# First attention stage: three pairs of probability tiles added by DMA, eight GpSimd additions, one block of row sums, and a new order within the steps

## The reference, cut to what matters

```python
kv = cond @ wkv.T + bkv                       # cond: (4, 1601, 512)
k, v = jnp.split(kv, 2, axis=-1)              # 16 heads of 32 columns
attn = jax.nn.softmax(jnp.einsum('bnhd,bmhd->bhnm', q, k) * scale, axis=-1)
o = jnp.einsum('bhnm,bmhd->bnhd', attn, v).reshape(B, N, C)
out = _qdq(o) @ _qdq(wp).T + bp               # _qdq: fake quantisation to int8
```

## Time and profile before

| | us |
|---|---|
| median of 3 runs (2567.41 to 2570.51) | 2568.93 |
| span of the profiled execution | 2568.4 |
| TensorE busy | 2506.9 (98%) |
| VectorE busy | 1786.5 (70%) |
| GpSimd busy | 1286.9 (50%) |
| ScalarE busy | 1223.6 (48%) |

### The profile page before, as it was taken

The page is one execution under the profiler, slowest core; times in us unless marked ns, Lnnn a source line. Parts: engine busy times, 40 slices in busy tenths (PEclk is TensorE's granted clock), DMA queues, the critical chain, the costliest instruction groups (busy, mean ns, idle before and its releaser), DMA issues. The chain is left out here.

```text
span 2568.4 us, 33913 instructions
## 1 busy us (share of the span) xinstructions
PE 2506.9 (98%) x13273; PEld 1626.8 (63%) x13288; DVE 1786.5 (70%) x2456; ACT 1223.6 (48%) x1853; POOL 1286.9 (50%) x340
## 2 busy tenths in 40 slices
PE   8999999999999999999998999999999999999998
PEld 8988888987545545555544787788533333335786
DVE  4554554556777767777774676664899999999873
ACT  4222313311666666666664232322688888886110
POOL 0000000000999999999993000000599999997310
PEclk9999999999999999999999999999999999999999
DMA  8677776655535345354323754443997777776300
GB/s 303 212 255 236 265 283 240 221 172 160 115 83 121 68 96 108 68 111 93 68 71 137 246 185 156 155 164 87 245 213 168 167 159 167 159 170 196 120 33 33
DMA packets 218865, 405.10 MB, mean 158 GB/s; under 512 B 18217, under 2 KB 94537, under 8 KB 218641
## 3 DMA queue, kind: packets, MB, share of 16 engines
q1 hardware_dynamic: 218704, 402.93, 56.8%
HBM read 260.63 MB, written 140.59 MB: 156 GB/s over the span
## 5 line engine op out<-in xcount | busy, mean ns | idle before, releaser
L1486 POOL TENSOR_TENSOR pooled<-pooled,probs 128x2048 f32<-128x2048 f32 x140 | 641.5, 4582 | 21.0 <-POOL pooled L1486 0.9
L1345 ACT ACTIVATE probs<-psum 128x512 f32<-128x512 f32 (+1 forms) x832 | 449.6, 600 | 333.6 <-PE psum L1231 328.4
L1372 DVE TENSOR_REDUCE win_max<-psum 128x1 f32<-128x802 f32 x480 | 454.3, 988 | 133.9 <-PE psum L1196 133.6
L2271 DVE TENSOR_SCALAR probs<-psum,bound 128x1024 f32<-128x1024 f32 (+1 forms) x416 | 499.0, 1275 | 31.5 <-POOL pooled L2303 21.3
L2246 ACT ACTIVATE probs<-probs 128x1024 f32<-128x1024 f32 (+1 forms) x416 | 437.6, 1059 | 82.5 <-DVE probs L2271 40.6
L2303 POOL TENSOR_TENSOR pooled<-pooled,probs 128x2048 f32<-128x2048 f32 x92 | 424.2, 4611 | 13.2 <-ACT probs L2246 1.0
L1231 PE MATMUL psum<-q_st,k_st 128*128 128x512 f32 (+1 forms) x832 | 318.7, 436 | 22.2 <-ACT probs L1345 15.6
L312 POOL TENSOR_TENSOR r_q<-ve_q,minus_half 128x4 f32<-128x4 f32 x8 | 9.1, 1133 | 611.3 <-DVE ve_q L256 611.3
L1196 PE MATMUL psum<-k_st,q_st 96*128 96x402 f32 x960 | 265.8, 358 | 0.9 <-DVE o_sb L1391 0.4
L1231 PEld LDWEIGHTS psum<-q_st,k_st 128*128 128x128 f32 (+1 forms) x832 | 149.4, 185 | 180.4 <-ACT probs L1345 130.6
L2214 PE MATMUL psum<-q_st,k_st 128*128 128x512 f32 (+1 forms) x832 | 251.6, 428 | 10.7 <-DVE probs L2271 9.6
(11 more groups left out here) (276 smaller groups left out, 4211.1 us busy)
## 6 DMA issues: line engine op xcount, KB each, us to landing
k_st<-k_hi SPq DMA_DIRECT2D x64, 801.0 KB, 10.6
k_st<-k_lo SPq DMA_DIRECT2D x48, 801.0 KB, 11.1
k_hi<-kt_hi SPq DMA_DIRECT2D x32, 801.0 KB
k_lo<-kt_lo SPq DMA_DIRECT2D x32, 801.0 KB
v_rows<-v_out SPq DMA_DIRECT2D x96, 256.0 KB
v_st<-v_rows SPq DMA_DIRECT2D x24, 768.0 KB
q_st<-q_hi SPq DMA_DIRECT2D x64, 256.0 KB, 8.4
w<-w_hi_d SPq DMA_DIRECT2D x64, 256.0 KB, 3.1
```

Of the source, the lines that this page charges most:

```text
L1345: A.activation(probs[i % NPROBS][0:rows, j, :], bank(score_banks.where["score", u, t, j])[0:rows, :], ACT.Exp, scale=1.0 / ROOT).then_inc( ...
L1372: V.tensor_reduce(win_max[:, r, j, c:c + 1], window(windows.where["max", u, i])[:, :, 0:MV], AX.XY, ALU.max).then_inc(max_done, 1)
L1486: G.tensor_tensor(pooled[u % 2][:], before[:], probs[tile(u, k) % NPROBS][:], ALU.add).then_inc(pool_added, 1)
L2271: V.tensor_scalar(probs[i % NPROBS][0:rows, half * W:half * W + W, :], window(("score", u, t, half))[0:rows], bound[0:rows, u // NG, t:t + 1],
```

## The change

Constants and buffers: `NPROBS` 9, one `pooled` buffer, three pairs of tiles.

```diff
-            NQ, NSLOT, NPROBS, LAG, TURN_AT, WINDOWS = 3, 3, 8, 2, 11, 3
-            LAST_SUM, CODES_AT, ROWS_AT = 1, 3, 5
+            NQ, NSLOT, NPROBS, LAG, TURN_AT, WINDOWS = 3, 3, 9, 2, 11, 3
+            SUM_AT, CODES_AT, ROWS_AT = 4, 3, 7
+            PAIRS, NADD, POOLED_LAST = ((0, 1), (4, 5), (8, 9)), 8, 7
-                pooled = [sbuf(f"pooled0{i}", [P, HPG, S]) for i in range(2)]
+                pooled = sbuf("pooled0", [P, HPG, S])
-                def three_banks(u, t):
-                    return 5 <= t < pooled_tiles(u) + LAG
+                def three_banks(u, t, j):
+                    if u == UNITS - 1 and t >= POOLED_LAST + LAG:
+                        return False
+                    return u == 0 or not (t == SUM_AT and j > 0 or t == SUM_AT + 1 and j == 0)
```

```diff
+                def released(u, t):
+                    if u == UNITS - 1:
+                        return pool_added, added(u, max(t, 1) if t else 3)
+                    if t == TT - 1:
+                        return lone_read, u + 1
+                    for p, (first, second) in enumerate(PAIRS):
+                        if t == second:
+                            return pair_landed(u, p)
+                    return pool_added, added(u, {0: 2, 2: 3, 3: 1, 4: 5, 6: 3, 7: 4, 8: 8, 10: 6, 11: 7}[t])
...
+                    def add_pair(u, p):
+                        d, (first, second) = len(PAIRS) * u + p, PAIRS[p]
+                        G.wait_ge(exp_done, score(u, second, HPG))
+                        G.wait_ge(tile_read, tile(u, first) + 1)
+                        if d >= 2:
+                            G.wait_ge(pair_added[d % 2], 16 * (d // 2))
+                        G.dma_start(flat(of(u, first)), flat(of(u, second)),
+                                    accum_op=ALU.add).then_inc(pair_added[d % 2], 16)
+                    def add(u, k, out, before, tile_of, ready):
+                        if k > 1:
+                            G.wait_ge(pool_added, added(u, k - 1))
+                        G.wait_ge(*ready)
+                        G.tensor_tensor(out[:], before[:], of(u, tile_of)[:], ALU.add).then_inc(pool_added, 1)
+                    add_pair(0, 0)
+                    for u in range(UNITS - 1):
+                        start = of(u, 2)
+                        G.wait_ge(tile_read, tile(u, 2) + 1)
+                        add(u, 1, start, start, 3, exps_of(u, 3))
+                        add(u, 2, start, start, PAIRS[0][0], pair_landed(u, 0))
+                        add_pair(u, 1)
+                        if u:
+                            G.wait_ge(summed, u)
+                        add(u, 3, pooled, start, 6, exps_of(u, 6))
+                        add(u, 4, pooled, pooled, 7, exps_of(u, 7))
+                        add(u, 5, pooled, pooled, PAIRS[1][0], pair_landed(u, 1))
+                        add_pair(u, 2)
+                        add(u, 6, pooled, pooled, 10, exps_of(u, 10))
+                        add(u, 7, pooled, pooled, 11, exps_of(u, 11))
+                        add(u, 8, pooled, pooled, PAIRS[2][0], pair_landed(u, 2))
+                        if u + 1 < UNITS - 1:
+                            add_pair(u + 1, 0)
```

The last unit keeps six additions of tiles 0 to 6, now starting in place in tile 0, and six tiles summed on PE. On PE the sums of a unit, tile 12 alone and `pooled`, stand in one block in step 4 of the next unit, and each kind of step has its own order; all but steps 1, 4, 10, 11 and 12 take the last branch:

```diff
+                    def sums(u):
+                        if u == 0:
+                            M.wait_ge(set_up, 1)
+                        take_den(u)
+                        lone_sum(u, TT - 1, start=True).then_inc(lone_read, 1)
+                        pooled_sum(u)
...
+                        scores(u, t, 0)
+                        if t == 1:
+                            maxima(0)
+                            scores(u, t, 1)
+                            maxima(1)
+                            scores(u, t, 2)
+                            scores(u, t, 3)
+                            maxima(2)
+                            values_behind()
+                        elif t == SUM_AT:
+                            maxima(0)
+                            if u:
+                                sums(u - 1)
+                            maxima(1)
+                            scores(u, t, 1)
+                            scores(u, t, 2)
+                            maxima(2)
+                            values_behind()
+                            scores(u, t, 3)
+                        elif t == TURN_AT - 1:
+                            maxima(0)
+                            scores(u, t, 1)
+                            scores(u, t, 2)
+                            maxima(1)
+                            scores(u, t, 3)
+                            values_behind()
+                        elif t == TURN_AT:
+                            values_behind()
+                            scores(u, t, 1)
+                            scores(u, t, 2)
+                            if u + 1 < UNITS:
+                                turn(u + 1)
+                            scores(u, t, 3)
...
+                        elif t == TURN_AT + 1:
+                            if u and t == close_at(u):
+                                closing(u - 1)
+                            scores(u, t, 1)
+                            scores(u, t, 2)
+                            scores(u, t, 3)
+                            values_behind()
+                        else:
+                            scores(u, t, 1)
+                            maxima(0)
+                            scores(u, t, 2)
+                            maxima(1)
+                            values_behind()
+                            maxima(2)
+                            if u and t == close_at(u):
+                                closing(u - 1)
+                            scores(u, t, 3)
```

More of the change, by code:

```diff
@@ L1158, in windows_at, with summed_alone, pair_landed, added @@
                     return range(min(t * WINDOWS, HPG * RT * 2), min((t + 1) * WINDOWS, HPG * RT * 2))
-                def pooled_tiles(u):
-                    return 11 if u < UNITS - 1 else 7
+                def summed_alone(u, t):
+                    return u == UNITS - 1 and t >= POOLED_LAST
+                def pair_landed(u, p):
+                    d = len(PAIRS) * u + p
+                    return pair_added[d % 2], 16 * (d // 2 + 1)
+                def added(u, k):
+                    return NADD * u + k
+                def pooled_whole(u):
+                    return added(u, NADD if u < UNITS - 1 else POOLED_LAST - 1)
+                def released(u, t):
[7 more added lines that the diff above has]
+                    return pool_added, added(u, {0: 2, 2: 3, 3: 1, 4: 5, 6: 3, 7: 4, 8: 8, 10: 6, 11: 7}[t])
                 def close_at(u):
-                    return TURN_AT + 1 if u < UNITS - 2 else 4
+                    return TURN_AT + 1 if u < UNITS - 2 else SUM_AT + 2
                 def kq_count(u):
                     return 32 * NQ * (u // NSLOT + (u % NSLOT == 2))
[L1173 to L1178, removed]
                 def steps():
@@ L1223, in scores @@
                         s, rows = u % NSLOT, TROWS[t]
-                        slot, free = score_banks.take(("score", u, t, j), among=(0, 1, 7) if three_banks(u, t) else (0, 1))
+                        slot, free = score_banks.take(("score", u, t, j), among=(0, 1, 7) if three_banks(u, t, j) else (0, 1))
                         if free:
@@ L1233, in scores, with take_den @@
                         score_banks.freed_by(exp_done, score(u, t, j) + 1)
+                    def take_den(u):
+                        _, free = score_banks.take(("sum", u), among=(7,))
+                        M.wait_ge(*free)
+                        score_banks.freed_by(den_copied, u + 1)
                     def values(u, t):
@@ L1244, in values, with lone_sum, pooled_sum @@
                                          pr[0:rows, j, :], start=(t == 0), stop=(t == TT - 1))
[L1245 to L1255, removed]
+                        m.then_inc(tile_read, 1)
+                        if summed_alone(u, t):
+                            if t == POOLED_LAST:
+                                take_den(u)
+                            lone_sum(u, t, start=t == POOLED_LAST)
+                    def lone_sum(u, t, start):
+                        rows, pr = TROWS[t], probs[tile(u, t) % NPROBS]
                         for j in range(HPG):
                             m = M.matmul(den[j * DH:(j + 1) * DH, :], ones[0:rows, :], pr[0:rows, j, :],
[L1258 to L1262, removed]
+                                         start=start, stop=False)
+                        return m
+                    def pooled_sum(u):
+                        M.wait_ge(pool_added, pooled_whole(u))
                         for j in range(HPG):
-                            m = M.matmul(den[j * DH:(j + 1) * DH, :], ones[:], pooled[u % 2][:, j, :], start=False, stop=True)
+                            m = M.matmul(den[j * DH:(j + 1) * DH, :], ones[:], pooled[:, j, :], start=False, stop=True)
                         m.then_inc(summed, 1)
+                    def sums(u):
```

(39 more changed lines are left out.)

21 lines of the change are left out of this document (12 added, 9 removed).

## The result

The changed kernel takes 2601.15 us (median of 4 runs, 2598.62 to 2603.72) against 2569.61 of the kernel before: ratio 1.0127, 95% interval 1.0113 to 1.0142. It is 31.5 us slower, where 37 us less were forecast. Its profiled execution has a span of 2599.3 us.

What follows compares the result with a forecast made beforehand. PE's order was taken to bound the kernel, then pair 0's loop at 44.5 us a unit: 14 x (47.04 - 44.5) = 35.6 plus 1.4 at the ends, 37 us less, median 2568.93 to 2532; range 2519 to 2590.

Steps and rivals of the forecast that it cites:

- What bounds the kernel: First attention: PE's own order sets the 47.04 us unit; POOL, ten additions taking 47.0, would be next.
- PE's unit of 44.2: PE per unit: 47.04 - 0.7 - 0.9 - 1.2 = 44.2 us, bounded by 43.0 and 45.6.
- Steps with three banks: PE's other steps, same products in a new order: 3.2 to 3.35 us each, gain 0.
- the order of steps 11 and 12: PE around turn and closing: values, turn or closing put between scores, saving 1.2 us a unit.
- The other terms: PE per unit: one group of sums less, -0.7 us; three banks nearly always, -0.9 us.
- POOL's additions and issues: POOL per unit: eight additions of 4.70 us, 37.6 in all, and three DMA issues taken as 1.0 each.
- The landing of a pair alone: A pair's adding transfer of 1,024 KB from SBUF to SBUF: 7.4 us, bounds 4.3 and 13.0.
- I let this overlap of 6 us cost 1.2: L = 8.6: Pair 0 beside loads of keys, queries and v: landing L grows from 7.4 to 8.6 us.
- The formula: Loop of pair 0: seven additions, three issues and the landing, 32.9 + 3i + L = 44.5 us a unit.
- Pairs 1 and 2 then are 2.0 early: Pairs 1 and 2 have two additions, 9.4 us, until wanted; with a 7.4 us landing, 2.0 early.
- C: Rival: slower, landings too late at second, fifth and eighth additions of each unit; 2607 us at L = 10.5; chance 0.25.
- D: Rival: DVE holds up POOL's three issues, pair 0's loop grows by 2.5 to 47.0 us; 2567, no change; chance 0.03.

Runs made afterwards that it cites:

- e7_order: Kernel before, with only PE's order of steps 11 and 12 in units 1 to 14 changed: 2567.89 us, ratio 1.0001.
- e10_late: Changed kernel, with SP starting all loads of a unit at score 0 of step 6 instead of step 0: 2593.88 us, ratio 1.0104.
- e8_first: Changed kernel, SP's loads grouped at steps 2, 6, 10; in unit 0 at 5 and 10, v of unit 1 in the last: 2525.05 us, ratio 0.9834.

## Why the prediction was wrong, step by step

- *What bounds the kernel.* Right. PE's order set 47.04, and POOL stood right behind it: `e7_order` shortens PE and gains nothing.
- *PE's unit of 44.2.* Right: 43.93 to 44.03 in every undisturbed unit of five kernels. Steps with three banks take 3.34 to 3.36 and gain nothing, as I had said, and the order of steps 11 and 12, taken as 1.2, is 1.4 in `e7_order`. The other terms were not measured one by one. Unit 14, 46.3, was missed: its steps 6 and 7 take 4.2 and 4.9 with the closing among the windows.
- *POOL's additions and issues.* Right in size: 8 x 4.6 and three issues of 0.88 (taken as 1.0), 39.5 a unit without the waits. The way from the issue ahead to the first addition was taken as 3.6; it is 3.7 in `e10_late`, and 6.0 in the long units, since PE runs at half clock there.
- *The landing of a pair alone.* Taken as 7.4, measured 6.9 to 7.0 as the page counts. The estimate from the Trainium skill's page "DMA: Bandwidth & Descriptors", section "Anatomy of one DMA", was 6.8 with the bytes counted twice, and this trace agrees with it for a pair alone; copying only, most take 4.5 to 4.7 against its 4.4. Its sum of a fixed cost and bytes has no term for other traffic.
- *"I let this overlap of 6 us cost 1.2: L = 8.6."* **This is the step that failed.** As the page counts, pair 0 landed in 13.9 to 14.2, so the overlap cost 6.9 to 7.2 over the 7.0 of a pair alone, and pair 2 in 15.3 to 16.2, 8 to 9 over it. Pair 0 was issued 13.4 us into the unit and not 15. I had treated a busy queue as a share of the bandwidth. What happens is that the first packet of the pair starts 5.5 us later, and until then it gets nothing (the fence of the 6.8 us). The formula also counts one issue too many, since the page's landing runs from the start of the issue. Without it and with 14.1, it gives 32.9 + 2 x 0.88 + 14.1 = 48.8 a unit, or 14 x 1.8 - 1.4 = 24 us above the kernel before; measured 31.5. In the forecast the issue too many had put this loop at 44.5 instead of 43.5, above PE's 44.2 instead of below. The loop was right, its term for the landing beside loads was mis-sized.
- *"Pairs 1 and 2 then are 2.0 early."* This followed from the same term. As pair 0 is late by 4.2, pair 2 slips from 1.4 us before the next unit to 2.7 us into it, meets the next loads, and is late by 6 itself. The formula has one late pair per unit; the kernel has two in every second unit, on average 98.7 for two units against the formula's 97.6.
- *The clock.* Left out. In each long unit it stands at 0.50 for 10.3 us [fence by stretch, third row], after PE had waited 7.85, and goes with 2.3 of the 10.8 us of unit 5; no run separates it from the wait.
- *Rivals.* C had the right sign and nearly the right size (2607 for a landing of 10.5), but I placed it at transfers that are slow by themselves, and argued against it that they stand mostly alone. Alone they land in 6.6. That its number comes near 2601 is luck: it has every pair late, in every unit and by less, where from unit 1 on pair 1 is never late and pairs 0 and 2 are late only in every second unit. D is not seen: 45 issues take 0.85 to 0.90 us each but for the first (1.05), beside DVE's work of 34 us a unit, most of it reductions out of PSUM; whether other work of DVE would hold an issue was not tested.

What is not settled: why about 16 packets of keys and queries for each DMA engine go first, a number that hardly depends on how much of the loads is still to come (issues 2.7 and 13.4 us into the unit have the same), and whether smaller packets of keys would hold a pair for less; no run changed their size without cutting the bytes. Beside the other loads of unit 14 (rows, tables and v) it started 3.7 us after the issue.

## What to carry to other kernels

A transfer on the critical path that shares the DMA engines with queued loads must be priced by which loads stand beside it in time, and not by its size over a share of the bandwidth; here moving the same loads into the gaps turned 31 us lost into 43 won. Where a second engine is full beside the one that bounds, relieving the first alone can gain nothing (`e7_order`). And a loop that closes over two engines with little room per turn (1.5 us here: POOL waits 4.37 for PE in `e8_first` and 2.8 where it sets the pace, in `e10_late`) makes one late event into a cycle: look at the periods of single units before the mean.

## What the runs showed of the hardware

- A pair issued by POOL beside SP's queued loads of keys and queries (packets of 6408 and 2048 B) had its first packet after 6.7 to 7.1 us, behind about 16 of them for each DMA engine; after 1.44 us alone, and after 1.5 to 2.2 beside v's packets of 512 B. Once started it held most of the engines: its queue's share was 81.6% and SP's 20.3% in the 6.1 us from 845.7 on, so the loads gave way only then.
- A packet of 8192 B from SBUF to SBUF takes 0.63 us when it adds and 0.32 when it copies, and POOL's issue 0.88 and 0.58 us.
- In PE's wait of 7.85 us at the sums the granted clock fell to 0.50 and stayed there for 10.3 us, 5.1 of them after PE worked again. In `e8_first`, the kernel with ordered loads, it stays at 1.00 through units 1 to 14.
